# Four banks for projections, one score buffer and an input normalised two groups ahead, in a fused patch-embedding, attention and expert kernel

## The reference, cut to what matters

```python
z = _layernorm(patches, ln1_g, ln1_b)
z = jnp.einsum('bnp,pe->bne', z, W_proj) + b_proj
z = _layernorm(z, ln2_g, ln2_b)
h = jnp.concatenate([cls_and_z_plus_pos_emb, txt], axis=1)
...
x = _layernorm(h)
q = jnp.einsum('bsd,hpd->bhsp', x, q_w) + q_b      # k and v alike
scores = jnp.einsum('bhqp,bhkp->bhqk', q, k) / jnp.sqrt(jnp.float32(P))
attn = jax.nn.softmax(scores, axis=2)
ctx = jnp.einsum('bhqk,bhkp->bqhp', attn, v)
h = h + ctx.reshape(B, S, H * P) @ l_w.T + l_b
...
h = h + expert_mixture(_layernorm(h))              # top 2 of 8, capacity limited
```

## Time and profile before

| what | value |
|---|---|
| median of 3 runs (lowest, highest) | 806.3 us (806.28, 808.27) |
| the profiled execution: its time, its span | 806.62 us, 805.0 us |
| PE, DVE, ACT, POOL busy | 712.6, 523.5, 294.1, 277.1 us |
| mean granted TensorE clock | 0.922 of 2.4 GHz |

### The profile page before, as it was taken

How to read it: one execution, slowest core, us unless ns; L and a number is a source line. 1 busy time by engine, 2 the same in 40 slices (tenths; PEclk the granted TensorE clock), 3 DMA queues, 4 the chain that set the end, 5 groups by cost and what they waited for, 6 DMA issues and landing times.

```text
span 805.0 us, 17117 instructions
## 1 busy us (share of the span) xinstructions
PE 712.6 (89%) x6527; PEld 665.0 (83%) x6527; DVE 523.5 (65%) x1143; ACT 294.1 (37%) x652; POOL 277.1 (34%) x293
## 2 busy tenths in 40 slices
PE   5979999979979899799799675089999999999996
PEld 4869888868868788688789565089999999999995
DVE  4992668867857768668668773255747657476561
ACT  3545554524425334245254220142524325243240
POOL 3671001030030120300201213634666665666615
PEclk9998999999989899989799756579999999999998
DMA  8530000000000000000000102414443454434312
GB/s 268 178 104 17 1 2 5 13 16 16 2 16 16 3 16 16 16 16 2 16 16 2 30 1 80 146 44 117 100 83 79 95 138 92 88 82 90 78 14 27
DMA packets 51266, 43.02 MB, mean 53 GB/s; under 512 B 25383, under 2 KB 44757, under 8 KB 51201
## 3 DMA queue, kind: packets, MB, share of 16 engines
q1 hardware_dynamic: 21729, 30.20, 12.2%
q0 software_dynamic: 29472, 11.90, 9.3%
HBM read 32.76 MB, written 10.25 MB: 53 GB/s over the span
## 4 chain that ended last, share of the span: by engine, by line
PE 57%; issue 25%; DVE 6%; DMA 5%; POOL 3%; ACT 2%; POOLq 1%; SPq 0%; DVEq 0%; ACTq 0%
PE shared L1310 9%; PE shared L1311 8%; PE shared L1312 8%; PE pair L1312 7%; PE pair L1310 7%; PE pair L1311 7%; DMA token_rows<-sent 4%; PE pair L1425 2%; PE ct_ps L1435 2%; PE vt_ps L1412 2%; PE ct_ps L1334 1%; PE shared L1471 1%; PE ct_ps L1564 1%; PE pair L1320 1%; POOL prob L617 1%
## 5 line engine op out<-in xcount | busy, mean ns | idle before, releaser
L775 ACT ACTIVATE qkv<-shared,bq_sb 128x276 f32<-128x276 f32 x192 | 93.7, 488 | 128.3 <-PE shared L1312 125.1
L1310 PE MATMUL shared<-xT_hi,wq_hi 128*128 128x276 f32 x384 | 127.0, 331 | 4.2 <-ACT x2T L813 1.5
L713 POOL DMA_INDIRECT out<-yrow,held x48 | 100.9, 2101 | 74.3 <-DVE yrow L1272 60.2
L1311 PE MATMUL shared<-xT_lo,wq_hi 128*128 128x276 f32 x384 | 114.0, 297 | 0.0
L1312 PE MATMUL shared<-xT_hi,wq_lo 128*128 128x276 f32 x384 | 113.4, 295 | 0.0
L885 ACT ACTIVATE act_f<-pair 128x348 f32<-128x348 f32 (+1 forms) x128 | 51.8, 457 | 97.3 <-PE pair L1312 97.3
L1310 PEld LDWEIGHTS shared<-xT_hi,wq_hi 128*128 128x128 f32 x384 | 75.2, 196 | 12.6 <-ACT x2T L813 2.6
L1310 PE MATMUL pair<-xe_hi,fc_hi 128*128 128x348 f32 (+1 forms) x256 | 82.7, 323 | 1.1 <-DVE xe_lo L1254 1.1
L1312 PE MATMUL pair<-xe_hi,fc_lo 128*128 128x348 f32 (+1 forms) x256 | 83.0, 324 | 0.0
L1311 PE MATMUL pair<-xe_lo,fc_hi 128*128 128x348 f32 (+1 forms) x256 | 82.9, 324 | 0.0
L696 POOL DMA_INDIRECT held<-token_rows,found_ix x48 | 67.9, 1414 | 26.7 <-issue 19.6
(11 more groups left out here) (179 smaller groups left out, 1737.2 us busy)
## 6 DMA issues: line engine op xcount, KB each, us to landing
raw_fc<-c_fc SPq DMA_DIRECT2D x8, 1024.0 KB, 7.2
raw_pj<-c_proj SPq DMA_DIRECT2D x8, 1024.0 KB, 7.5
qkv<-w_qkv SPq DMA_DIRECT2D x6, 512.0 KB, 7.4
qkv<-patches SPq DMA_DIRECT2D x6, 384.0 KB, 4.8
token_rows<-sent POOLq DMA_DIRECT2D x8, 285.7 KB, 7.1
out<-h SPq DMA_DIRECT2D x8, 276.0 KB
more_patches<-patches SPq DMA_DIRECT2D x3, 384.0 KB, 9.0
qkv<-w_l SPq DMA_DIRECT2D x1, 1024.0 KB, 7.8
```

The lines of the kernel that those rows point to most:

```text
L713: pool.indirect_dma_start(out, bass.IndirectOffsetOnAxis(ap=xg[p][0:n, t, D:D + 1].bitcast(U32), axis=0), yrow[p][0:n, t, :], None, bounds ...
L775: act.activation(qkv[(st.i + shift) % 2][:, c, :], shared[bank][:, 0:GT], ACT.Identity, bias=bq_sb[:, c:c + 1]).then_inc(s_free[bank], 1)
L1310: pe.matmul(dst, l_hi, r_hi, start=(first and n == 0), stop=False)
L1311: pe.matmul(dst, l_hi, r_lo, start=False, stop=False)
```

## The change

- `BANKS = 4`: the second pair buffer becomes two more shared banks; uses go round four banks. `taken` looks at four.
- One score buffer: `take_max` and `score` use `pair[0]` always, and `score(u+1)` waits for the subtraction of unit u, where it waited for that of u-1.
- Input two groups ahead: `xn` of group 1 is made before the steps; in step i, `norm_in` for group i+2 stands in unit 1 ahead of `weigh_values(1)`, `norm_in_end` in unit 4 behind `weigh_values(4)`. On POOL `add_positions` (group i+2) now comes before `root_in` (group i+2).
- `put_place` moves behind `low_ctx(7)` and `take_max` of the next unit 0.
- `sweep(..., GROUPS, GROUPS, 0, 2)` writes all eight steps out, on all five engines.

```diff
+BANKS = 4
-    return {use: (n % 2, n // 2 + 1) for n, use in enumerate(order)}
+    return {use: (n % BANKS, n // BANKS + 1) for n, use in enumerate(order)}
-        shared = [... for i in range(2)]
+        shared = [... for i in range(2)] + [pair[1][:, i, :] for i in range(2)]
...
             def stage_b(st):            # POOL
-                if st.i + 1 < GROUPS:
-                    root_in(st, 1)
                 if st.i + 2 < GROUPS:
                     add_positions(st, 2)
+                    root_in(st, 2)
...
             def take_max(st, u):        # DVE
-                sc = pair[u % 2][0:SEQ, :, 0:UP * SEQ]...
+                sc = pair[0][0:SEQ, :, 0:UP * SEQ]...
...
+            norm_in(Step(0), 1)         # DVE, before the steps
+            norm_in_end(Step(0), 1)
             take_max(Step(0), 0)
...
-                    if u == 0 and more:
-                        norm_in(st, 1)
+                    if u == 1 and st.i + 2 < GROUPS:
+                        norm_in(st, 2)
                     if u == 2 and before:
                         residual(st, -1)
                     weigh_values(st, u)
-                    if u == 0 and more:
-                        norm_in_end(st, 1)
+                    if u == 4 and st.i + 2 < GROUPS:
+                        norm_in_end(st, 2)
...
-                    if u == 7 and before:
-                        put_place(st, -1)
                     if u == UNITS - 1:
                         low_ctx(st, u)
                     if u + 1 < UNITS:
                         take_max(st, u + 1)
                     elif more:
                         take_max(Step(st.i + 1, st.k, st.span), 0)
+                    if u == 7 and before:
+                        put_place(st, -1)
...
             def score(st, u):           # PE
-                wait(pe, s_sub, st, lambda i: UNITS * i + u - 1)
+                wait(pe, s_sub, st, lambda i: UNITS * i + u)
-                        done = pe.matmul(pair[u % 2][0:SEQ, e, ...
+                        done = pe.matmul(pair[0][0:SEQ, e, ...
...
-            sweep(pe, stage_b, GROUPS, 2, 2, 2)
+            sweep(pe, stage_b, GROUPS, GROUPS, 0, 2)
```

More of the change, by code:

```diff
@@ L135, in sweep @@
         body(Step(i))
-    with eng.Fori(0, (n - head - tail) // span) as k:
-        for i in range(head, head + span):
-            body(Step(i, k, span))
+    if n > head + tail:
+        with eng.Fori(0, (n - head - tail) // span) as k:
+            for i in range(head, head + span):
+                body(Step(i, k, span))
     for i in range(n - tail, n):
@@ L206, in program @@
         pair = [ctx.enter_context(nc.psum_tensor(f"pair{i}", [128, 2, 512], F32)) for i in range(2)]
-        shared = [ctx.enter_context(nc.psum_tensor(f"shared{i}", [128, 512], F32)) for i in range(2)]
+        shared = [ctx.enter_context(nc.psum_tensor(f"shared{i}", [128, 512], F32)) for i in range(2)] + [pair[1][:, i, :] for i in range(2)]
         vt_ps = ctx.enter_context(nc.psum_tensor("vt_ps", [128, 512], F32))
@@ L358, in program @@
             sem(n) for n in ("s_wp_hi", "s_wp_lo", "s_wq_hi", "s_wq_lo", "s_wq_lo2", "s_wl_hi", "s_wl_lo", "s_gb", "s_cs", "s_sums"))
-        s_full = [sem(f"s_full{i}") for i in range(2)]
-        s_free = [sem(f"s_free{i}") for i in range(2)]
+        s_full = [sem(f"s_full{i}") for i in range(BANKS)]
+        s_free = [sem(f"s_free{i}") for i in range(BANKS)]
         s_h, s_n_ln, s_xn, s_xT_hi, s_xT_lo = (sem(n) for n in ("s_h", "s_n_ln", "s_xn", "s_xT_hi", "s_xT_lo"))
@@ L467, in stage_b @@
                 sp.dma_start(out_tile[:, bass.ds(g * TPG, TPG), :], h2[:, :, :]).then_inc(s_h2_out, 16)
-            sweep(sp, stage_b, GROUPS, 1, 3, 2)
+            sweep(sp, stage_b, GROUPS, GROUPS, 0, 2)
             def load_fc(e):
@@ L681, in _ @@
             add_positions(Step(0), 1)
+            root_in(Step(0), 1)
             rows_here(PT - 1)
-            sweep(pool, stage_b, GROUPS, 2, 2, 2)
+            sweep(pool, stage_b, GROUPS, GROUPS, 0, 2)
             root_mid(Step(GROUPS), -1)
@@ L848, in stage_b @@
                         put_gap(st, -1)
-            sweep(act, stage_b, GROUPS, 2, 2, 2)
+            sweep(act, stage_b, GROUPS, GROUPS, 0, 2)
             put_y(Step(GROUPS), -1)
@@ L1012, in take_max @@
             def take_max(st, u):
-                sc = pair[u % 2][0:SEQ, :, 0:UP * SEQ].rearrange("s e (q k) -> s e q k", k=SEQ)
+                sc = pair[0][0:SEQ, :, 0:UP * SEQ].rearrange("s e (q k) -> s e q k", k=SEQ)
                 tp = top[:, :].rearrange("s (e q) -> s e q", e=2)
@@ L1202, in stage_b @@
                         low_ctx(st, u)
-            sweep(dve, stage_b, GROUPS, 2, 2, 2)
+            sweep(dve, stage_b, GROUPS, GROUPS, 0, 2)
             last = Step(GROUPS)
@@ L1375, in taken @@
             def taken(st, kind, shift, blocks):
-                for bank in range(2):
+                for bank in range(BANKS):
                     mine = [c for c in blocks if USE[(kind, st.i + shift, c)][0] == bank]
@@ L1424, in score @@
                         c, r = 2 * (UP * h + q), slice(HD * e, HD * (e + 1))
-                        done = pe.matmul(pair[u % 2][0:SEQ, e, q * SEQ:(q + 1) * SEQ], qkv[st.i % 2][r, c + 1, s],
+                        done = pe.matmul(pair[0][0:SEQ, e, q * SEQ:(q + 1) * SEQ], qkv[st.i % 2][r, c + 1, s],
                                          qkv[st.i % 2][r, c, s], start=True, stop=True)
```

## The result

The changed kernel takes 773.3 us (median of 4 runs, 771.51 to 775.8), the kernel before 806.3 us (median of 4, 805.72 to 808.27) on the same chip. The ratio is 0.9588, 95% interval [0.9566, 0.9609]: 4.1% faster. Forecast were 774.0 us and 763 to 785. The profiled execution of the changed kernel took 771.51 us, with a span of 769.7. The total is right to a thousandth; the terms behind it are not, as the experiments show.

A forecast was written before the change was run, and what follows sets the result against it. PE was taken to be bound by its stall for xn behind POOL's queue and the slow clock after it. 41.1 + 1.2 + 1.5 - 4.0 - 7.0 = 32.8 us off 806.6 gave 774, range 763 to 785.

The forecast's parts named there:

- rival 1: New waits behind norm_in and at the turns of steps are hidden and cost nothing: 763 us; chance 0.16.
- Input ahead, +42.3 less 4.0 for norm_in: Steps 0 to 6: without the stall for xn, gains of 41.1 and 1.2 us; norm_in in unit 1 costs 4.0.
- Four banks, +1.5: PE's short waits for a bank: the 0.25 us behind x2T, six times, goes away, gaining 1.5 us.
- norm_in in unit 1, -4.0: norm_in ahead of weigh_values(1) delays context 2: 0.8 us in steps 0 and 1, 0.6 in steps 2 to 5.
- One score buffer, -7.0: At each of seven turns of a step PE waits 1.0 us for the subtraction: cost 7.0 us.
- rival 4: One score buffer ties PE to DVE in every unit, 1.0 us in each of 57 others: 831 us; chance 0.03.
- Met waits, 0: Up to 256 more waits on PE from taken looking at four banks, each already met: no cost taken.
- rival 3: Already met waits on PE cost 0.03 us each, +7.7 us: 781 us; chance 0.06.
- POOL's margin, 0.9 us: POOL finishes add_positions for group i+2 0.9 us before DVE comes to norm_in in unit 1.
- Rival 2: The wait moves to POOL: DVE's norm_in waits for the positions, +5.2 to +9 us: 779 to 783; chance 0.20.
- The loop: The 2.7 us idle at the hardware loop's turn goes when written out, priced within the 41.1 us of steps 1 to 6.
- Rival 5: Nothing gained: fetching straight code brings idle times and slow clock in every step, 4 us x 8: about 806; chance 0.02.

The follow-up runs named there:

- Experiment 2: Kernel before with the input two groups ahead and all eight steps written out; two banks and two score buffers stay: 789.29 us, ratio 0.9772.
- experiment 4: Changed kernel with the input normalised one group ahead, as before the change: 799.53 us, ratio 0.9871.
- experiment 8: Kernel before with input two groups ahead, steps written out, norm_in behind take_max in unit 1; two banks, two score buffers: 772.86 us, ratio 0.9576.
- experiment 3: Kernel before with input two groups ahead, steps written out and one score buffer; two banks, put_place ahead of the maximum: 801.13 us, ratio 0.9897.
- experiment 10: Changed kernel with put_place back ahead of low_ctx(7) and the maximum: 777.06 us, ratio 0.9629.
- experiment 5: Changed kernel with norm_in moved behind take_max(2) of unit 1: 763.01 us, ratio 0.9442.
- experiment 9: Changed kernel with each wait that taken issues written twice, 232 more instructions: 773.73 us, ratio 0.9581.
- experiment 6: Changed kernel with score(1) of each step between the two halves of the output projection: 776.06 us, ratio 0.9615.
- experiment 1: Kernel before with the input two groups ahead alone; two banks, two score buffers and the loop stay: 800.96 us, ratio 0.9904.
- experiment 7: Changed kernel with norm_in behind take_max(2) of unit 1 and score(1) between the halves of the output projection: 754.47 us, ratio 0.9343.

## Why the prediction was right, and where its steps were wrong

**What bounds it: right.** The stall for `xn` behind POOL's queue was what made steps 2 to 6 long, and it went. Steps 2 to 5 have the forecast length, 47.3 us for 47 to 48; step 6 is 1 us below its 47. That the length comes out is partly luck: each step begins from 1.45 us less than I had (rival 1, below), the turn costs the 1.0 forecast, and the place of `norm_in` costs 1.5 where I had 0.6.

**Input ahead, +42.3 less 4.0 for norm_in: wrong when taken alone.** The step that failed is "without the stall each is step 1". Experiment 2 does all of this part and gains 0.0228, 18 us, not 38; added last it gains 23 (experiment 4). Behind the stall for `xn` stood a second wait, on the same DVE queue, that the stall had hidden in four steps of five: the bank of `tabulate` has to be read by `add_table`, and with two banks PE is there 3.3 us too early. Step 1 could not show it, because it has no `tabulate`; step 4 did, with 1.29 us, and the prediction makes nothing of it. With `norm_in` in unit 1 the 1.29 becomes 3.3 (experiments 8 and 2). I had added `tabulate` as 0.5 us of PE work, and not as a bank that someone has to empty.

**Four banks, +1.5: wrong by more than a factor of ten.** The step is "PE's waits for a bank are short: 0.35 and 0.25 us". They were short in a trace in which PE stood still for 5 us in each step just before, so that DVE and ACT were never behind. From experiment 3 to the change, 0.0309 or 25 us are gained by the banks and the place of `put_place` together; the latter is 3.3 (experiment 10), so four banks are worth some 22 us, if the two add up. The sum came out by luck, because both errors are about 20 us: I gave to the input ahead what four banks earn. The 22 hold for this place of `norm_in` alone: with it in the good one the banks bring 11 us after the turns' 7.5 are paid (experiment 8), some 18 in all. "Four banks are also the cover for ACT" had the right thought, for the wrong reader and without a price.

**norm_in in unit 1, -4.0: right in kind, wrong in place and size.** In step 1 it costs at contexts 1 and 2 (0.62 and 0.63 us, for a forecast of 0.8), in steps 2 to 5 at the table's bank (1.28 us, for 0.6 at context 2). In the windows that is 7.4 us, by the medians 10 and by the ratios 12 (experiment 5).

**One score buffer, -7.0: right.** Seven turns of 1.07 or 1.08 us. Within the steps no score waits, so rival 4 is out.

**put_place, moved for nothing: right**, and not moving it costs 3.3 us (experiment 10). **Met waits, 0: right**, and rival 3 is out (experiment 9).

**POOL's margin, 0.9 us: 0.44.** POOL's `prob` grew by 0.58 us beside `in_row`. By the rule of the Trainium skill that the prediction named (SBUF — State Buffer, Who interferes with whom), a VectorE instruction with two SBUF inputs and a GpSimd one that reads SBUF exclude each other; the 0.86 us without `in_row` beside it and 1.44 with it agree. `in_row` had 0.72 us left when `prob` started. `in_row` itself takes 0.88 us either way. Rival 2 did not hold, by less than half a microsecond, and experiment 6 shows it at work as soon as DVE comes earlier. The prediction read `xn` beside the addition as each engine holding up the other; the addition takes 1.79 us there and 1.81 without `xn` beside it, so only DVE was held up.

**The loop: undervalued.** I had priced it inside the 41.1, where its own 2.7 us stood. With the input ahead, writing it out gave 11.7 us (experiments 1 and 2), 8.2 of them in the steps of the loop. The idle time and the slow step behind it are seen; 1.5 us in step 1 are a fall of the clock outside the loop, and the rest is open. **Rival 5** is out: straight code in every step was no slower.

**Rival 1, 763 us**, was that both new waits cost nothing. They do cost, but moving one of them gives 763.0 and moving both gives 754.5: below the 763. A step there takes 44.66 us where I had 45.61 and 0.5 for `tabulate`; of the 1.45 us, 0.56 are PE's idle time in the earlier trace rows, and 0.85 the busy time that four banks save (experiments 5 and 8).

## What to carry to other kernels

A wait that is removed uncovers the next one on the same queue: before pricing a stall at its full length, look who was idle during it, and ask of every shared buffer used behind it whether its reader would still be in time. Waits for buffers that are short in a trace with a big stall say nothing of how many buffers are needed without it. And work moved early on an engine's queue goes behind whatever somebody waits for: `norm_in` needed only to be a step ahead, and behind `take_max` it left no wait on PE (experiment 7).

## What the runs showed that was not expected

- A wait of TensorE of about 1.3 us can go either way. Behind its four for the table, 1.28 or 1.29 us, the change's trace shows the full clock each time; in experiment 9 the clock fell behind two of four (0.79 on average from 182 to 190 us, 1.6 us lost). Behind 1.78 us it fell in experiment 10 (0.59 from 171 to 174.5), behind 1.60 to 1.64 it did not; behind 1.94 and more, in steps 1 to 6, it fell in every trace, to 0.51 in experiment 6. The 1.21 us wait of step 7 has the full clock behind it in the kernel before, the change and experiments 4, 8 and 9, and 0.66 over the next 5 us in experiments 1, 3, 5 and 10.
- The turn of the hardware loop costs more than its idle time: 3.2 us idle in experiment 1, and 8.2 us less in the four steps of the loop when they are written out.
- One small operation of POOL, 92x3 numbers, takes 0.86 us (experiment 10), and 1.44 with a DVE operation of two inputs beside it (the change).
